# A projection whose next layer norm runs ahead of the group's differences, and an attention stack loaded under two semaphores

## The chip, the cores and the metric

The kernel runs on one core of one Trainium2 chip. A core has five engines that run their own instruction streams: TensorE (PE, with its weight loads shown as PEld), VectorE (DVE), ScalarE (ACT), GpSimd (POOL) and SyncE (SP), which in this kernel issues nearly all DMA transfers. They meet only through semaphores. The metric is the time of one execution in microseconds; less is better. Before the change, three executions took 4418.20, 4414.44 and 4430.01 us, a median of 4418.2 us.

## The reference

The input is x with 4096 rows (2 sequences of 2048) of 256 numbers. Two layers follow one another.

```python
x = x + attention(layernorm(x))      # 16 heads of 16, with relative-position keys and values
x = x + ffn(layernorm(x))            # itself: layernorm, plain attention, layernorm, top-2 of 8 experts
def _layernorm(x, axis=-1, eps=1e-05):
    m = jnp.mean(x, axis=axis, keepdims=True)
    v = jnp.var(x, axis=axis, keepdims=True)
    return (x - m) / jnp.sqrt(v + eps)
q = proj(Wq, bq); k = proj(Wk, bk); v = proj(Wv, bv)          # x @ W.T + b, 16 heads
scores = jnp.einsum('bqhd,bkhd->bhqk', q, k) / np.sqrt(DK)     # plain attention
attn = jax.nn.softmax(scores, axis=-1)
```

## The kernel before, in words

The program is a chain of stages, each a block of its own with its own semaphores; between two blocks the engines meet and SP clears the semaphores of the old one. The order is: first projection (`rel_projection`), attention with relative positions, middle stage, plain attention (`plain_attention`), routing, experts. Inside a block the order of each engine's work is written out by hand, and nothing reorders it.

**First projection.** The 4096 rows are taken in 8 groups of 512 (g = 0 to 7). For each group TensorE
transposes the normalised rows h into psT (L1505), ACT copies them to hT (L1467), TensorE multiplies them with the query and key weights into four banks of psU (L1522) and with the value weights into the two halves of psV (L1537). Queries and keys are stored as two numbers each, a rounded high part and the rest. ACT makes the six high parts of a group (L1483, output rel_parts), one or two for each bank; DVE makes the six differences, value minus high part (L1412, also rel_parts). The differences free the psU banks for the next group. DVE also adds the bias to both halves of psV (L1423, output rel_vout). SP stores each of the six outputs after its difference (L1346), the values after the second vout (L1352), and right behind the first store of group g it loads x for group g+2 (L1350).

The layer norm of the next group is a generator on DVE (`layer_norm`, L91), stepped from between the differences. Its steps are: statistics of four tiles (L94); three sums (L98); mean and square (L101, L102); variance (L106); plus epsilon (L110); after ACT's square root (`root`, L1461) the reciprocal (L113); and the four tiles of h (L119). A tuple says how many steps run behind each difference, (2, 2, 1, 1, 1, 0), and on ACT `root(g + 1)` stands behind the fourth high part.

TensorE's order in a group is: psU in four banks, first half of psV, the transposes of group g+1 (they wait for h), second half of psV. In group 0 the second half of psV also waits for rel_ekt, a copy (L1428) that DVE makes between its two vout additions.

**Plain attention.** 32 heads run one after the other. A head's queries and keys lie in a stack of 128 partitions: the lower rows (from partition 0, 48 of them) serve the first pass, in which TensorE forms scores (L459) only so that DVE can take their maxima (L370); the upper rows (from partition 64, 50 of them) serve the second pass, the fills (L484), whose results ACT turns into exponentials (L433). SP loads a stack with twelve transfers of 128 KB (`load_stacks`, L275): six for the lower rows, then six for the upper. All twelve count up one semaphore of the stack's slot, `s_qz[slot]`; there are four slots. TensorE waits for it once, ahead of the first score of a head. At the start SP issues the stacks of heads 0 and 1, then the values of all heads, then head 2.

Of the kernel before, what the change touches and what calls it, by code (L numbers as in the profile page):

```python
# [16 lines left out]
DK = D // NH  # L17
NB = 2
S = 2048
# [8 lines left out]
NG = T // G  # L28
# [95 lines left out]
U = 4  # L124
HEADS = NB * NH
# [36 lines left out]
def plain_attention(nc, ident, sel, qd, kd, vd, den_d, rec_d, ot_rows):  # L162
# [19 lines left out]
    with ExitStack() as ctx:  # L182
# [28 lines left out]
        psO = ps("psO", [P, G])  # L211

        s_one, s_init, s_vall, s_v = sem("s_one"), sem("s_init"), sem("s_vall"), sem("s_v")
        s_qz = [sem(f"s_qz{i}") for i in range(U)]
        s_a, s_am, s_nm, s_mt, s_mh, s_mr, s_mq = (sem(n) for n in
            ("s_a", "s_am", "s_nm", "s_mt", "s_mh", "s_mr", "s_mq"))
        s_fl, s_ex, s_us, s_oev = (sem(n) for n in ("s_fl", "s_ex", "s_us", "s_oev"))
# [3 lines left out]
        ctx.callback(clear_semaphores, nc, sems)  # L221
        blk = ctx.enter_context(nc.Block())

        NLD = 4 * len(Q2)
        NINIT = 5
        lead = 3

# [34 lines left out]
        @blk.sync  # L262
        def _(sp):
            def load_stacks(t, p):
                b, h = head(t)
                slot = p % U
                row, col = ready(sp, h * DK), ready(sp, b * S)
                s_us.wait(sp, STEPS * (t - 3))
                for half in range(2):
                    if half and t < U:  # L270
                        s_one.wait(sp, t + 1)
                    for parts, dst, src in ((Q2, qs, qd), (K2, zs, kd)):
                        for i, part in enumerate(parts):
                            at = 64 * half + i * DK
                            sp.dma_start(dst[at:at + DK, slot, :].bitcast(F32),  # L275
                                         src[part, bass.ds(row, DK), bass.ds(col, S)]).then_inc(s_qz[slot].h, 16)

            def send_m(t, p):
                s_mr.wait(sp, t + 1)
                for m in range(NP2):  # L280
                    at = 64 + PR + m
                    sp.dma_start(qs[at:at + 1, p % U, :].bitcast(F32), mrow[:, m, :].bitcast(F32)
                                 ).then_inc(s_mq.h, 16)

            def spread_reciprocals(t, n):

                s_nf.wait(sp, t + 1)
                for c in range(4):
                    row = 32 * c + DK
                    sp.dma_start(den_d[:, c * G:(c + 1) * G].rearrange("(a u) q -> a u q", a=1),  # L290
                                 ob[row:row + 1, :, :]).then_inc(s_dw.h, 16)
                s_dw.wait(sp, 64 * (n + 1))
                sp.dma_start(den[:, :], den_d.rearrange("u (x j) -> (u x) j", j=U * S // P)).then_inc(s_dr.h, 16)
                s_rec.wait(sp, n + 1)
                sp.dma_start(rec_d.rearrange("u (x j) -> (u x) j", j=U * S // P), rec[:, :]).then_inc(s_rw.h, 16)
                s_rw.wait(sp, 16 * (n + 1))
                for c in range(4):
                    sp.dma_start(recb[32 * c:32 * c + DK, :, :],
                                 bass.AP(rec_d.tensor, rec_d.offset + c * G, [[0, DK], [S, U], [1, G]])
                                 ).then_inc(s_rr.h, 16)  # L300

            def store_o(t, n):

                b, h = head(t + HEADS - U)
                row, col = ready(sp, h * DK), ready(sp, b * S)
                s_ml.wait(sp, n + 1)
                for c in range(4):
                    sp.dma_start(ot_rows[bass.ds(row, U * DK), bass.ds(col + c * G, G)].rearrange(
                        "(u d) q -> d u q", u=U), done[32 * c:32 * c + DK, :, :]).then_inc(s_ob.h, 16)

            give_credits(sp, sems)
            for t in range(lead):
                load_stacks(t, t)
                if t == 1:
                    for b in range(NB):
                        sp.dma_start(vall[:, b, :, :], vd[b * S:(b + 1) * S, :].rearrange("(z p) c -> p z c", p=P)
                                     ).then_inc(s_vall.h, 16)
            send_m(0, 0)
            for it in range(HEADS // U):
                for p in range(U):  # L320
                    t = U * it + p
                    if t + lead < HEADS:
                        load_stacks(t + lead, p + lead)
                    if p == 0:
                        spread_reciprocals(t, it)
                    if t + 1 < HEADS:
                        send_m(t + 1, p + 1)
                    if p == 0:
                        store_o(t, it)
            for k in range(U):  # L330
                s_qz[k].wait(sp, 16 * NLD * HEADS // U)
            s_mq.wait(sp, 16 * NP2 * HEADS)
            spread_reciprocals(HEADS, HEADS // U)
            store_o(HEADS, HEADS // U)
            s_ob.wait(sp, 64 * (HEADS // U + 1))
# [116 lines left out]
        def _(pe):  # L452
            def scores(a, half, w, p, loaded):

                k, a = p + a // 32, a % 32
                if a == 0 and half == 0:
                    s_qz[k % U].wait(pe, 16 * NLD * loaded(k))
                i, e = a // 2, 2 * (a % 2) + half
                last = pe.matmul(psA[w][:, half, :], qs[0:PR, k % U, i * P:(i + 1) * P],  # L459
                                 zs[0:PR, k % U, e * G:(e + 1) * G], start=True, stop=True)  # L460
                if half:
                    last.then_inc(s_a.h, 1)
# [13 lines left out]
            def fill(t, p, i):  # L476
                if t == HEADS:
                    return
                s_ex.wait(pe, BANKS * t + before(i) + 1)
                if i == 0:  # L480
                    s_mq.wait(pe, 16 * NP2 * (t + 1))
                c, z = i // 16, i % 16
                at = 64
                pe.matmul(psS[:, slot(i), :], zs[at:at + PR + NP2, p % U, z * P:(z + 1) * P],  # L484
                          qs[at:at + PR + NP2, p % U, c * G:(c + 1) * G], start=True, stop=True).then_inc(s_fl.h, 1)
# [784 lines left out]
def rel_projection(nc, A, ident, sel, masks, e_stack, evc, ev_side, q2, kl2, kr2, v_rows):  # L1270
# [10 lines left out]
    with ExitStack() as ctx:  # L1281
# [112 lines left out]
        def _(dve):  # L1394
# [12 lines left out]
            for g in range(NG):  # L1407
                q = g % 2
                ahead = normalise(dve, g + 1) if g + 1 < NG else iter(())
                for o, (m, col, _, _) in enumerate(OUTS):  # L1410
                    s_hi.wait(dve, NO * g + BY_UNIT[m])
                    dve.scalar_tensor_tensor(out=parts[:, q, o, 1, :], in0=psU[:, m, :], scalar=cols[:, col:col + 1],  # L1412
                                             in1=parts[:, q, o, 0, :], op0=ALU.add, op1=ALU.subtract
                                             ).then_inc(s_lo.h, 1)
                    for _ in zip(range((2, 2, 1, 1, 1, 0)[o]), ahead):
                        pass
                for v in range(2):
                    s_v.wait(dve, 2 * g + v + 1)
                    if v == 0:
# [32 lines left out]
        @blk.scalar  # L1452
        def _(act):
            def weight(i, bank):
                s_wt.wait(act, i + 1)
                act.activation(wt[:, :, i * D:(i + 1) * D], bank.rearrange("p (c n) -> p c n", c=CH), ACT.Copy
                               ).then_inc(s_wc.h, 1)

            def root(g):
                s_ve.wait(act, g + 1)  # L1460
                act.activation(sd[:, g % 2, :], ve[:, g % 2, :], ACT.Sqrt).then_inc(s_sd.h, 1)  # L1461

            def stationary(g):
                s_v.wait(act, 2 * (g - 1))
                for c in range(CH):
                    s_t.wait(act, CH * g + c + 1)
                    act.activation(hT[:, g % 2, c, :], psT[:, c, :], ACT.Copy).then_inc(s_hT.h, 1)  # L1467

            weight(0, psU[:, 2, :])
            root(0)  # L1470
            weight(1, psU[:, 3, :])
            stationary(0)
            weight(2, psV[:, 0, :, :].rearrange("p a c -> p (a c)"))
            for g in range(NG):
                q = g % 2
                for o, (m, col, _, _) in enumerate(OUTS):
                    s_u.wait(act, 4 * g + m + 1)
                    if g == 0 and o == 0:
                        s_bias.wait(act, 16 * 6)
                    if g == 0 and col == 4:  # L1480
                        s_col.wait(act, 4)
                    s_po[q][o].wait(act, 16 * (g // 2))
                    act.activation(parts[:, q, o, 0, :], psU[:, m, :], ACT.Identity, bias=cols[:, col:col + 1]  # L1483
                                   ).then_inc(s_hi.h, 1)
                    if o == 3 and g + 1 < NG:
                        root(g + 1)
                if g + 1 < NG:
                    stationary(g + 1)

# [1123 lines left out]
```

## Time and profile before

| quantity | value |
|---|---|
| median of three executions | 4418.2 us |
| the profiled execution | 4430.09 us, span 4428.4 us |
| first projection, in the span | 0 to about 128 us |
| start of plain attention (first load to first score) | 2231.16 to 2245.63 us |
| PE, DVE, ACT, POOL busy over the span | 90%, 79%, 68%, 33% |

A row of the timeline reads: start, duration, engine, line of the program, operation, tile written and tiles read, shapes, how many instructions are merged into the row; in brackets the time for which the engine stood idle before it and what it waited for. The busy shares are means over stages with different limits; what the change is worth is read from the two stretches in the table.

### The profile page before, as it was taken

The numbers are of one execution on the slowest core, as the hardware profiler recorded it, in microseconds if no ns is written. First come the engines' busy times: TensorE is split into PE (matmuls) and PEld (weight loads), VectorE is DVE, ScalarE is ACT, GpSimd is POOL, SyncE is SP. The second block draws the span as 40 slices with busy tenths as digits, with TensorE's granted clock in tenths as the row PEclk, the third lists the DMA queues.
The fourth block names the chain that finished last, engine by engine and source line by source line (L and its number), as shares of the span: only waits on it lengthen the run. The fifth ranks groups of instructions, "written<-read, shape, count | busy, mean of one in ns | idle before, by whom it ended". The sixth has DMA issues, their size and how long they took to land. (4 is left out here: it accounts for less than half of the span.)

```text
span 4428.4 us, 77243 instructions
## 1 busy us (share of the span) xinstructions
PE 4001.6 (90%) x26592; PEld 2106.5 (48%) x26592; DVE 3490.8 (79%) x6304; ACT 2991.0 (68%) x5821; POOL 1445.9 (33%) x1405
## 2 busy tenths in 40 slices
PE   7699999999999999996879999999999996689997
PEld 4344444444444444443533333333333332589997
DVE  6688888888888888862769888988888881577775
ACT  3067777777777777783218888888888884256664
POOL 0255666666666656662100000000000000613222
PEclk9589999999999999998959999999999997689998
DMA  7656666666666767654662323233333302666664
GB/s 269 179 142 164 150 163 161 163 154 168 155 159 159 168 159 165 161 116 129 234 120 40 54 30 54 40 44 45 44 44 46 43 13 70 176 207 174 177 170 115
DMA packets 486195, 556.39 MB, mean 126 GB/s; under 512 B 60260, under 2 KB 426836, under 8 KB 476524
## 3 DMA queue, kind: packets, MB, share of 16 engines
q1 hardware_dynamic: 465980, 526.94, 49.1%
q0 software_dynamic: 19824, 24.52, 3.5%
q8 instruction: 211, 3.46, 0.4%
q14 instruction: 180, 1.47, 0.1%
HBM read 347.67 MB, written 206.76 MB: 125 GB/s over the span
## 5 line engine op out<-in xcount | busy, mean ns | idle before, releaser
L1096 ACT ACTIVATE ra_p<-ra_psS 128x512 f32<-128x512 f32 x2048 | 1089.6, 605 | 368.2 <-PE ra_psS L1173 266.1
L370 DVE TENSOR_REDUCE pa_pm<-pa_psA 128x2 f32<-128x1024 f32 x1024 | 1208.3, 1219 | 140.7 <-PE pa_psA L459 140.7
L1007 DVE TENSOR_REDUCE ra_pm<-ra_psA 128x1 f32<-128x896 f32 x1024 | 1113.5, 1087 | 205.9 <-PE ra_psA L1131 190.4
L433 ACT ACTIVATE pa_p<-pa_psS 128x512 f32<-128x512 f32 x2048 | 1063.5, 604 | 249.4 <-PE pa_psS L484 245.0
L484 PE MATMUL pa_psS<-pa_qs,pa_zs 50*128 50x512 f32 x2048 | 793.4, 464 | 77.3 <-ACT pa_p L433 62.8
L459 PE MATMUL pa_psA<-pa_zs,pa_qs 48*128 48x512 f32 x2048 | 797.2, 472 | 44.2 <-DMA pa_zs<-k_halves 23.8
L1131 PE MATMUL ra_psA<-ra_zs,ra_qs 48*128 48x512 f32 x2048 | 736.0, 455 | 44.9 <-DVE ra_pm L1009 23.8
L1173 PE MATMUL ra_psS<-ra_qs,ra_zs 50*128 50x512 f32 (+3 forms) x2176 | 713.8, 411 | 32.4 <-ACT ra_p L1096 17.5
L484 PEld LDWEIGHTS pa_psS<-pa_qs,pa_zs 50*128 50x128 f32 x2048 | 342.2, 185 | 626.2 <-ACT pa_p L433 606.7
L1204 PE MATMUL ra_psO<-ra_p,ra_vs 128*32 128x512 f32 (+3 forms) x6400 | 566.6, 459 | 0.0
L495 PE MATMUL pa_psO<-pa_p,pa_vs 128*32 128x512 f32 x4096 | 548.0, 607 | 0.0
L1173 PEld LDWEIGHTS ra_psS<-ra_qs,ra_zs 50*128 50x128 f32 x2176 | 353.4, 187 | 395.4 <-ACT ra_p L1096 307.7
L459 PEld LDWEIGHTS pa_psA<-pa_zs,pa_qs 48*128 48x128 f32 x2048 | 346.6, 189 | 214.0 <-DVE pa_pm L370 160.5
L1131 PEld LDWEIGHTS ra_psA<-ra_zs,ra_qs 48*128 48x128 f32 x2048 | 328.5, 194 | 166.4 <-DVE ra_pm L1009 85.0
L343 POOL COPY pa_vs<-pa_vall 128x256 f32<-128x256 f32 x32 | 12.7, 399 | 1057.1 <-PE pa_psO L495 1023.7
L947 POOL TENSOR_TENSOR ra_blk<-ra_blk 128x508 f32<-128x508 f32 x128 | 162.9, 1273 | 461.6 <-DMA ra_blk<-window_rows 456.6
L2353 PE MATMUL mo_psH<-mo_hp,mo_w_parts 128*128 128x384 f32 x1392 | 285.3, 341 | 5.9 <-DVE mo_w_parts L2439 5.9
L2367 PE MATMUL mo_psY<-mo_w_parts,mo_hid_parts 128*128 128x256 f32 x2088 | 283.6, 281 | 0.6 <-DVE mo_hid_parts L2509 0.6
L2324 POOL DMA_INDIRECT acc_rows<-mo_y,mo_ids x87 | 154.5, 1776 | 387.7 <-DVE mo_y L2494 370.0
L2367 PEld LDWEIGHTS mo_psY<-mo_w_parts,mo_hid_parts 128*128 128x128 f32 x2088 | 272.1, 189 | 4.9 <-DVE mo_hid_parts L2509 1.1
L1204 PEld LDWEIGHTS ra_psO<-ra_p,ra_vs 128*32 128x32 f32 x6400 | 194.9, 109 | 131.2 <-ACT ra_p L1096 82.5
L1102 ACT ACTIVATE ra_sw<-ra_sw,ra_nm 128x256 f32<-128x256 f32 x512 | 242.8, 526 | 0.0
(247 smaller groups left out, 4977.9 us busy)
## 6 DMA issues: line engine op xcount, KB each, us to landing
relative_rows<-ra_rst SPq DMA_DIRECT2D x128, 512.0 KB, 4.0
ra_blk<-window_rows SPq DMA_DIRECT2D x128, 512.0 KB
mo_w_raw<-ffn_W SPq DMA_DIRECT2D x58, 1024.0 KB, 5.5
ra_zs<-k_halves SPq DMA_DIRECT2D x192, 248.0 KB, 7.4
ra_dl<-relative_rows SPq DMA_DIRECT2D x128, 256.0 KB, 5.4
window_rows<-ra_pc SPq DMA_DIRECT2D x128, 256.0 KB, 4.8
pa_qs<-q_halves SPq DMA_DIRECT2D x192, 128.0 KB, 6.3
pa_zs<-k_halves SPq DMA_DIRECT2D x192, 128.0 KB, 6.9
```

Source lines behind the costliest of these rows:

```text
L370: dve.reduce_max(pm[:, par, 2 * a:2 * a + 2], psA[w][:, :, :], AX.X).then_inc(s_am.h, 1)
L433: act.activation(pr[:, i % NPR, :], psS[:, slot(i), :], ACT.Exp).then_inc(s_ex.h, 1)
L459: last = pe.matmul(psA[w][:, half, :], qs[0:PR, k % U, i * P:(i + 1) * P], zs[0:PR, k % U, e * G:(e + 1) * G], start=True, stop=True)
L484: pe.matmul(psS[:, slot(i), :], zs[at:at + PR + NP2, p % U, z * P:(z + 1) * P], qs[at:at + PR + NP2, p % U, c * G:(c + 1) * G], start=True ...
L495: last = pe.matmul(psO[32 * m:32 * m + 32, :], vs[:, p % 2, 4 * (k % 4) + m, :], pr[:, (4 * k + m) % NPR, :], start=k % 4 == 0, stop=k % 4 ...
L1007: dve.reduce_max(pm[:, q, i, 2 * left:2 * left + 1], psA[w][:, lo:lo + 2 * G - P], AX.X).then_inc(s_far.h, 1)
L1096: act.activation(dst, psS[:, slot(i), :], ACT.Exp if kind == "E" else ACT.Copy).then_inc(s_cp.h, 1)
L1131: last = pe.matmul(psA[w][:, half * G:(half + 1) * G], qs[0:PR, q, i * P:(i + 1) * P], zs[0:PR, q, at:at + G], start=True, stop=True)
L1173: last = pe.matmul(dst[:, lo:hi], zs[at:at + PR + NP2, q, z * P:(z + 1) * P], qs[at:at + PR + NP2, q, c * G + lo:c * G + hi], start=True, ...
L1204: last = pe.matmul(psO[32 * m:32 * m + 32, lo:hi], v[:, z, :], pr[:, (4 * k + m) % NPR, lo:hi], start=n == 0, stop=n == 3, tile_position=( ...
L2353: last = pe.matmul(psH[:, u % 3, 0:BT], w1[:, q, x, c, f * P:(f + 1) * P], hp[:, q, z, c, :], start=c == 0 and m == 0, stop=c == CH - 1 an ...
L2367: last = pe.matmul(psY[:, j, 0:D], hid[:, x, u % NHID, j * P:(j + 1) * P], w2[:, q, z, f, :], start=f == 0 and m == 0, stop=f == FC - 1 an ...
```

## The change

In `rel_projection` the numbers of layer-norm steps become (5, 2, 0, 0, 0, 0) and the stepping moves ahead of each difference: five steps ahead of the first, the last two ahead of the second. On ACT `root(g + 1)` moves ahead of the six high parts. In `plain_attention` the semaphores `s_qz` are replaced by `s_qa` for a slot's lower rows and `s_qe` for its upper rows, each counting six transfers. TensorE waits for `s_qa` ahead of a head's first score and for `s_qe` ahead of its first fill. SP waits for both at the end.

```diff
-        s_qz = [sem(f"s_qz{i}") for i in range(U)]
+        s_qa, s_qe = ([sem(f"{n}{i}") for i in range(U)] for n in ("s_qa", "s_qe"))
-        NLD = 4 * len(Q2)
+        NLD = 2 * len(Q2)
...
-                                         src[part, bass.ds(row, DK), bass.ds(col, S)]).then_inc(s_qz[slot].h, 16)
+                                         src[part, bass.ds(row, DK), bass.ds(col, S)]).then_inc((s_qe if half else s_qa)[slot].h, 16)
...
-                s_qz[k].wait(sp, 16 * NLD * HEADS // U)
+                s_qa[k].wait(sp, 16 * NLD * HEADS // U)
+                s_qe[k].wait(sp, 16 * NLD * HEADS // U)
...
                 if a == 0 and half == 0:
-                    s_qz[k % U].wait(pe, 16 * NLD * loaded(k))
+                    s_qa[k % U].wait(pe, 16 * NLD * loaded(k))
...
                 if i == 0:
+                    s_qe[p % U].wait(pe, 16 * NLD * (t // U + 1))
                     s_mq.wait(pe, 16 * NP2 * (t + 1))
...
                 for o, (m, col, _, _) in enumerate(OUTS):
+                    for _ in zip(range((5, 2, 0, 0, 0, 0)[o]), ahead):
+                        pass
                     s_hi.wait(dve, NO * g + BY_UNIT[m])
                     dve.scalar_tensor_tensor(out=parts[:, q, o, 1, :], in0=psU[:, m, :], scalar=cols[:, col:col + 1],
                                              in1=parts[:, q, o, 0, :], op0=ALU.add, op1=ALU.subtract
                                              ).then_inc(s_lo.h, 1)
-                    for _ in zip(range((2, 2, 1, 1, 1, 0)[o]), ahead):
-                        pass
...
             for g in range(NG):
                 q = g % 2
+                if g + 1 < NG:
+                    root(g + 1)
                 for o, (m, col, _, _) in enumerate(OUTS):
...
-                    if o == 3 and g + 1 < NG:
-                        root(g + 1)
```

On VectorE, group 1 of the first projection stands so before the change (L1412 is a difference, L94 to L119 are the layer norm of group 2):

```order
L1412 SCALAR_TENSOR_TENSOR rel_parts<-rel_psU,rel_cols,rel_parts 128x512
L94 BN_STATS rel_stats<-rel_x 128x6 x4
L98 TENSOR_TENSOR rel_moments<-rel_stats 128x4 x3
L1412 SCALAR_TENSOR_TENSOR rel_parts<-rel_psU,rel_cols,rel_parts 128x512
L101 TENSOR_SCALAR rel_mean<-rel_moments 128x4
L102 SCALAR_TENSOR_TENSOR rel_moments<-rel_moments 128x4
L106 SCALAR_TENSOR_TENSOR rel_moments<-rel_moments 128x4
L1412 SCALAR_TENSOR_TENSOR rel_parts<-rel_psU,rel_cols,rel_parts 128x512
L110 TENSOR_SCALAR rel_ve<-rel_moments 128x4
L1412 SCALAR_TENSOR_TENSOR rel_parts<-rel_psU,rel_cols,rel_parts 128x512
L113 RECIPROCAL rel_rs<-rel_sd 128x4
L1412 SCALAR_TENSOR_TENSOR rel_parts<-rel_psU,rel_cols,rel_parts 128x512
```

The same group on VectorE after the change (a difference is now L1416, the vout addition L1425):

```order
L94 BN_STATS rel_stats<-rel_x 128x6 x4
L98 TENSOR_TENSOR rel_moments<-rel_stats 128x4 x3
L101 TENSOR_SCALAR rel_mean<-rel_moments 128x4
L102 SCALAR_TENSOR_TENSOR rel_moments<-rel_moments 128x4
L106 SCALAR_TENSOR_TENSOR rel_moments<-rel_moments 128x4
L110 TENSOR_SCALAR rel_ve<-rel_moments 128x4
L1416 SCALAR_TENSOR_TENSOR rel_parts<-rel_psU,rel_cols,rel_parts 128x512
L113 RECIPROCAL rel_rs<-rel_sd 128x4
L119 TENSOR_SCALAR rel_h<-rel_x,rel_mean,rel_rs 128x256 x4
L1416 SCALAR_TENSOR_TENSOR rel_parts<-rel_psU,rel_cols,rel_parts 128x512 x5
L1425 TENSOR_TENSOR rel_vout<-rel_psV,rel_v_bias 128x512 x2
```

The four tiles of h, which stood behind the fifth difference, now stand behind the first; five differences and the vout additions follow in a row.

On ScalarE, groups 0 and 1 before the change (L1483 is a high part, L1461 the square root, L1467 the copy of hT):

```order
L1483 ACTIVATE rel_parts<-rel_psU,rel_cols 128x512 x4
L1461 ACTIVATE rel_sd<-rel_ve 128x4
L1483 ACTIVATE rel_parts<-rel_psU,rel_cols 128x512 x2
L1467 ACTIVATE rel_hT<-rel_psT 128x512 x2
L1483 ACTIVATE rel_parts<-rel_psU,rel_cols 128x512 x4
L1461 ACTIVATE rel_sd<-rel_ve 128x4
```

And after it (the square root is now L1463, a high part L1487, the copy of hT L1469):

```order
L1463 ACTIVATE rel_sd<-rel_ve 128x4
L1487 ACTIVATE rel_parts<-rel_psU,rel_cols 128x512 x6
L1469 ACTIVATE rel_hT<-rel_psT 128x512 x2
L1463 ACTIVATE rel_sd<-rel_ve 128x4
L1487 ACTIVATE rel_parts<-rel_psU,rel_cols 128x512 x6
```

The square root has moved from behind the fourth high part to ahead of the first. In plain attention no instruction that computes or transfers is moved.

## Rows read from the trace of the kernel before

**Rows 1.** Page, the head and one of the costliest groups: idle before it, and releaser.
```profile
span 4428.4 us, 77243 instructions
...
L459 PE MATMUL pa_psA<-pa_zs,pa_qs 48*128 48x512 f32 x2048 | 797.2, 472 | 44.2 <-DMA pa_zs<-k_halves 23.8
```

**Rows 2.** Waits, 0 to 170 us: waiter, releaser, total us, times, longest.
```profile
PE rel_psT L1505 <- DVE rel_h L119: 18.0, 8, 2.4
```

**Rows 3.** Timeline of PE, group 4 of the first projection.
```profile
71.20 7.03 PE L1522 MATMUL rel_psU<-rel_hT,rel_w_qkv_t 128*128 128x512 f32 x16
78.07 1.89 PE L1537 MATMUL rel_psV<-rel_w_qkv_t,rel_hT 128*128 128x256 f32 x8
82.20 1.09 PE L1505 MATMUL rel_psT<-ident,rel_h 128*128 128x128 f32 x8 [2.24 <-DVE rel_h L119]
83.13 1.89 PE L1537 MATMUL rel_psV<-rel_w_qkv_t,rel_hT 128*128 128x256 f32 x8
84.86 7.03 PE L1522 MATMUL rel_psU<-rel_hT,rel_w_qkv_t 128*128 128x512 f32 x16
```

**Rows 4.** Timeline of the other engines in the same group.
```profile
71.40 0.69 DVE L1423 TENSOR_TENSOR rel_vout<-rel_psV,rel_v_bias 128x512 f32<-128x512 f32 x1 [1.66 <-PE rel_psV L1537]
...
73.12 0.69 ACT L1483 ACTIVATE rel_parts<-rel_psU,rel_cols 128x512 fp32r<-128x512 f32 x1 [2.74 <-PE rel_psU L1522]
73.84 0.75 DVE L1412 SCALAR_TENSOR_TENSOR rel_parts<-rel_psU,rel_cols,rel_parts 128x512 fp32r<-128x512 f32 x1 [1.75 <-ACT rel_parts L1483]
...
75.02 0.47 SPq L1350 DMA_DIRECT2D rel_x<-attn_x  x1
...
76.55 1.27 ACT L1483 ACTIVATE rel_parts<-rel_psU,rel_cols 128x512 fp32r<-128x512 f32 x2 [1.03 <-PE rel_psU L1522]
...
82.95 1.08 ACT L1467 ACTIVATE rel_hT<-rel_psT 128x512 f32<-128x512 f32 x2 [2.88 <-PE rel_psT L1505]
```

**Rows 5.** Timeline, middle stage: a layer norm that no difference interrupts.
```profile
2196.26 0.69 DVE L1735 TENSOR_TENSOR mid_vout<-mid_psV,mid_v_bias 128x512 f32<-128x512 f32 x1 [1.91 <-PE mid_psV L1821]
...
2199.31 0.21 ACT L1744 ACTIVATE mid_sd<-mid_ve 128x4 f32<-128x4 f32 x1 [3.72 <-DVE mid_ve L110]
2199.43 1.25 ACT L1768 ACTIVATE mid_parts<-mid_psU,mid_cols 128x512 fp32r<-128x512 f32 x2
2200.13 0.75 DVE L1722 SCALAR_TENSOR_TENSOR mid_parts<-mid_psU,mid_cols,mid_parts 128x512 fp32r<-128x512 f32 x1 [0.85 <-ACT mid_parts L1768]
...
2201.00 1.38 DVE L119 TENSOR_SCALAR mid_h<-mid_x,mid_mean,mid_rs 128x256 f32<-128x256 f32 x4
2202.30 0.74 DVE L1722 SCALAR_TENSOR_TENSOR mid_parts<-mid_psU,mid_cols,mid_parts 128x512 fp32r<-128x512 f32 x1
```

**Rows 6.** Timeline, group 0 of the first projection: the two halves of psV.
```profile
21.55 1.89 PE L1537 MATMUL rel_psV<-rel_w_qkv_t,rel_hT 128*128 128x256 f32 x8
...
27.02 3.37 PE L1537 MATMUL rel_psV<-rel_w_qkv_t,rel_hT 128*128 128x256 f32 x8 [0.24 <-DVE rel_ekt L1428]
```

**Rows 7.** Windows (ending: granted clock, DMA share, GB/s) and the landing of x.
```profile
57.50:71.20 13.70, 11.46 (x41) 6.85 (x41) 8.89 (x24) 5.09 (x9) 0.00 (x0) 1.00 0.88 316
...
66.00:68.00 2.00, 0.30 (x2) 0.00 (x0) 1.55 (x4) 0.41 (x1) 0.00 (x0) 1.00 1.05 408
...
DMA to landing us min/median/max: 4.7/4.7/6.4
```

**Rows 8.** Plain attention's start: the six lower-row loads, and the first score.
```profile
2231.16 1.83 SPq L275 DMA_DIRECT2D pa_qs<-q_halves  x3
...
L275 SPq DMA_DIRECT2D pa_zs<-k_halves x3: 419/420/420, 2233.0 to 2234.0; - x3
...
DMA to landing us min/median/max: 3.0/4.1/5.5
...
2245.63 2.07 PE L459 MATMUL pa_psA<-pa_zs,pa_qs 48*128 48x512 f32 x4 [23.84 <-DMA pa_zs<-k_halves]
```

**Rows 9.** Windows, plain attention: where the granted clock rises.
```profile
2315.00:2325.00 10.00, 9.63 (x52) 3.00 (x54) 6.63 (x7) 6.07 (x13) 0.00 (x0) 0.74 0.01 3
```

## The prediction

> **What bounds the kernel now.** I read the page first: the span, and the group of first-pass score matmuls, whose PE idle time names a DMA as its longest releaser: 23.8 us behind the load of the key stack [rows 1]. That is one wait, at the start of plain attention, where PE, DVE and ACT all stand still. The page's slices show the first projection only as four blurred columns, so I asked for the waits of 0 to 170 us. There TensorE waits 18.0 us in 8 waits for the normalised tile h that VectorE writes [rows 2]. The timeline of TensorE alone shows where [rows 3]: a group runs from one start of the psU matmuls to the next, 71.20 to 84.86, so 13.66 us. In it PE does psU (6.87 us to the next start), half of psV, then stands 2.24 us for h, then transposes (0.93 us to the next start) and the second half of psV (1.73 us). A first half of psV also takes 1.73, so the work in a group is 6.87 + 1.73 + 0.93 + 1.73 = 11.26 us, and 2.40 us of the period is the hole before the transposes. PE is at the full clock there (1.00, which is 2.4 GHz) [rows 7]. The last wait in this stage is thus h, which VectorE finishes late because its six steps stand between six differences. The rest of the program (both attentions, the middle stage, routing, the experts) is touched only through the starting time of plain attention.
>
> **Part 1, the steady group.** The edit adds and removes no arithmetic. It moves the layer norm of group g+1 on DVE ahead of the differences of group g, and the square root on ACT from behind the fourth high part to ahead of the first. I lay out a new group from the start of psU as zero.
> The trace of before has a layer norm that runs undivided, in the middle stage [rows 5]: from the start of the vout addition (2196.26) to the square root on ACT is 3.05 us, and the next ACT high part starts at 3.17. In the projection vout starts at +0.20 [rows 4], so now the root starts at +3.25 and the first high part at +3.37. Before it was at +1.92 (73.12). ACT therefore loses 1.45 us at the front: the price of the edit, because high parts 1 to 6 are queued behind a root that waits for DVE. The first difference follows the high part by 0.72 [rows 4]: +4.09. From a difference to h is 0.87 (2200.13 to 2201.00), h takes 1.38, the next difference starts 2.17 after the first [rows 5]: h is complete at +6.34, the second difference is at +6.26. Differences in a row cost 0.74 each (durations 0.75 with the overlap of starts), so the last starts at +9.2, vout at +9.9, and DVE is done at +10.6. The last two high parts need the fourth bank: banks come 1.715 us apart (76.55 less 73.12, halved), so at +7.07, and two high parts take 1.27: +8.3, ahead of the fifth difference (+8.5). ACT is not late.
> PE ends the first half of psV at +8.60 and finds h ready since +6.34, so the 2.24 us wait is gone with 2.26 to spare. It transposes to +9.53. ACT copies hT from 0.75 after the transposes start, for 1.08 [rows 4], so to +10.43; PE ends psV at +11.26 and finds hT ready. The next psU bank needs only the first difference. DVE meets the next vout at +11.46 with 0.9 us in hand. What is late next is nothing but PE itself: period 11.26, gain 2.40 in each of groups 1 to 6: **14.4 us**. Group 7 has no layer norm behind it and stays.
>
> **Group 0.** Here the second half of psV also waits for a copy (rel_ekt) that stands behind the differences and vout. The fourth bank reaches ACT about 0.2 us after psV's start at 21.55 [rows 6], two high parts end at 23.0, difference 5 at 23.05, difference 6 at 23.8, vout at 24.45, the copy at 25.1 to 25.4. PE starts at 25.4 where it started at 27.02: **1.6 us**. That half of psV took 3.37 us for eight matmuls where 1.89 is usual [rows 3, 6], so PE fell to its lower clock level (1.2 GHz) behind its pause. If the shorter pause keeps it at the upper level, another 1.5 us comes. I take nothing for that, since the only row for this place is the slow one, and keep 1.5 for the low end of the range. DVE still has its constants to make at the start of group 1 (about 2 us); h is then ready at about +8.4, still ahead of +8.60.
>
> **The transfers.** Each group issues seven stores and one load of 512 KB, 4.19 MB. SP passes the x load right behind the first store, now at +5.3 (difference 1 plus the 1.18 us from 73.84 to 75.02) instead of +3.8, and the next statistics want it at +11.26 + 0.20 + 0.69 = +12.15: 6.9 us, where landings take 4.7 to 6.4 [rows 7]. Before, it had some 13 us. The stores no longer have gaps between them but come in a burst. Windows in which the queue is full show 408 GB/s at a share of 1.05 [rows 7]; at 400 GB/s the group needs 10.5 us of the 11.26. It just fits, so I charge nothing.
>
> **Part 2, the stacks.** PE's first score waited for all 12 loads of head 0 and now waits for the 6 of the lower rows. SP issues in the same order. The sixth load is issued at 2234.0 and landed 5.5 us later, at 2239.5 (it is the largest of the six landings); PE started at 2245.63 [rows 8]. That is 6.0 us earlier, less 0.2 that I allow for four more semaphores that SP credits ahead of the loads (no row has a price for one; it is bounded below by nothing and above by 1 us): **5.8 us**. Everything behind it moves along: VectorE sets the pace of the first turns, and its own memsets are over by then. The upper rows are wanted only by the first fill some 56 us later, and have landed. The added wait stands once a head on PE ahead of a fill, with the scores, fills and weighings queued behind it, and its load is three heads old: nothing, at most 0.04 us in each of 32 heads, 1.3 us. Clearing four more semaphores and four more waits of SP at the end: 0.3 us.
>
> **The sum.** 14.4 + 1.6 + 5.8 - 0.3 = 21.5 us. The profiled execution took 4430.1 us (1.7 beside its span), which would become 4408.6. It was the slowest of the executions shown, 12 us above their median of 4418.2 us, so I set the forecast against the median: **4397 us**. The executions of one kernel lie 16 us apart, which is nearly the size of the effect.
>
> **A limit on transfers.** The shares read otherwise than the full windows: over a whole group 316 GB/s at a share of 0.88 is 359 GB/s at a full share [rows 7]. By that a group needs 4.19/0.359 = 11.7 us, the queue becomes the bound at 11.7 instead of 11.26, and groups 1 to 6 give 2.0 each, 11.7 in all. The sum is then 18.8 and the time 4399.
> The Trainium skill, "DMA: Bandwidth & Descriptors", section "Where 436 GB/s comes from", says that a transfer between HBM and SBUF is bound by about 358 GB/s for each core, below the 435 GB/s of the fabric. By that rule the limit above holds and the group takes 11.7 us; the two-microsecond windows of this trace go above it, and an average of the changed stage over some groups will tell.
>
> **Rivals.** (a) The forecast, 4388 to 4405: 0.60. (b) The transfers bind as above, 4399: 0.15. For it is the mean share, against it the full windows. (c) The stacks bring nothing net: PE runs at the lower level from its first score to about 2318, where the window 2315 to 2325 shows 0.74 [rows 9]. Fills begin 56 us after the first score, and PE is dense from then. If the rise stays at its old time while work comes 5.8 us sooner, 5.8 us more of dense work runs at half speed, which costs 2.9, and a like shift at the start of relative attention up to as much. Gain 16, time 4402: 0.15. (d) The projection does not do what it says, since DVE, not PE, sets the period: it has 0.9 us in hand, and if every semaphore hop in the longer chain vout, statistics, root, high part, difference, h costs more than in the middle stage it can need 13 us. Then only part 2 and about 1 us are left: 4412: 0.06. (e) Slower: the x load comes late. Its deadline is 6.9 us after issue, PE has 2.26 more, so it hurts from 9.1 us of landing, and groups 2 to 6 (those fed by the five loads issued inside the loop) only equal the old period at 11.5. The whole kernel is slower from 13.4 us. At 18 us, four times today's 4.7, each of the five groups loses 18 - 11.5 = 6.5 us, 32 in all, against 9.5 gained elsewhere: 4441. The burst of stores in one queue speaks for it, the shorter queue that a longer period would leave speaks against it: 0.04.
>
> **Numbers.** What a measurement of this kernel can tell from no change is about 0.5%, 22 us, and the forecast of 21.5 stands almost on it. Of (a) 0.37 lies beyond it, with the clock's 1.5 us and the spread of executions, of the others 0.05, by the spread alone: faster 0.42, within 0.54, slower 0.04. The range is 4387 (all of it, the 1.5 us and a fast median) to 4412 (case d); it leaves out (e) and the tails of (a).
>
> **What would show it.** In the profile after: psU starts of groups 1 to 7 11.3 us apart; no wait of rel_psT for rel_h; the ACT root before all six high parts, its wait for ve grown to about 1.5 us or more; the first difference about 4.1 us after psU starts; DMA share near 1 in the stage; the last matmul of the projection near 106.5 us instead of 122.7; the first score of plain attention 8.7 us after its first load is issued, instead of 14.5 (2231.16 to 2245.63) [rows 8]. The prediction is wrong if the period stays above 12, if the first score comes later than 10 us behind the first load, or if later stages give the time back.

## The result, and the profile after

Twelve executions of the changed kernel took 4403.2 us in the median (4380.46 to 4426.22), twelve of the kernel before 4434.5 (4414.44 to 4460.02). The ratio is 0.993 with a 95% interval of 0.9909 to 0.9951: 31 us faster, 22 to 40. The forecast was 21.5 us, and 4397 us for the time. A second comparison on another chip (below) gave 0.9949, 22.6 us, and the places in the trace add up to 22.0. So the mechanism was sized rightly, and some 9 us of the first comparison belong to neither part of the change. The time itself came out near the forecast partly by luck: the median of before that it started from, 4418.2 us of three executions, is 16 us below that of twelve, and the gain was 10 us above the forecast. Where such scatter comes from is the second half of this text; for the first comparison itself it can't be shown, since the executions of the kernel before there have, but for one, no clock on record. The profiled execution has a span of 4401.8 us, 26.6 less than before.

First the projection. Timeline of PE, group 4 of the changed kernel, answering to [rows 3]:

```profile
60.62 7.03 PE L1524 MATMUL rel_psU<-rel_hT,rel_w_qkv_t 128*128 128x512 f32 x16
67.48 1.89 PE L1539 MATMUL rel_psV<-rel_w_qkv_t,rel_hT 128*128 128x256 f32 x8
69.21 1.04 PE L1507 MATMUL rel_psT<-ident,rel_h 128*128 128x128 f32 x8
70.08 1.89 PE L1539 MATMUL rel_psV<-rel_w_qkv_t,rel_hT 128*128 128x256 f32 x8
71.81 7.03 PE L1524 MATMUL rel_psU<-rel_hT,rel_w_qkv_t 128*128 128x512 f32 x16
```

The bracket behind the transposes is gone: PE no longer waits for h here. From psU to psU it is 11.19 us instead of 13.66. The other engines in the same group, answering to [rows 4]:

```profile
63.23 1.41 DVE L94 BATCH_NORM_STATS2 rel_stats<-rel_x 128x6 f32<-128x256 f32 x4 [1.72 <-DMA rel_x<-attn_x]
...
65.69 0.20 ACT L1463 ACTIVATE rel_sd<-rel_ve 128x4 f32<-128x4 f32 x1 [5.89 <-DVE rel_ve L110]
65.80 3.56 ACT L1487 ACTIVATE rel_parts<-rel_psU,rel_cols 128x512 fp32r<-128x512 f32 x6
66.50 0.75 DVE L1416 SCALAR_TENSOR_TENSOR rel_parts<-rel_psU,rel_cols,rel_parts 128x512 fp32r<-128x512 f32 x1 [0.85 <-ACT rel_parts L1487]
...
67.38 1.38 DVE L119 TENSOR_SCALAR rel_h<-rel_x,rel_mean,rel_rs 128x256 f32<-128x256 f32 x4
...
67.69 0.81 SPq L1352 DMA_DIRECT2D rel_x<-attn_x  x1
68.67 3.38 DVE L1416 SCALAR_TENSOR_TENSOR rel_parts<-rel_psU,rel_cols,rel_parts 128x512 fp32r<-128x512 f32 x5
...
71.97 1.28 DVE L1425 TENSOR_TENSOR rel_vout<-rel_psV,rel_v_bias 128x512 f32<-128x512 f32 x2
```

The root follows the start of the statistics by 2.46 us and the first difference by 3.27; the forecast, from the middle stage's undivided norm, had 2.36 and 3.20. But the statistics themselves start at +2.61 and not at +0.9, since DVE waits 1.72 us for x. h is thus ready at +8.14, 0.45 us ahead of PE instead of 2.26. In group 5 nothing is left:

```profile
78.98 1.38 DVE L119 TENSOR_SCALAR rel_h<-rel_x,rel_mean,rel_rs 128x256 f32<-128x256 f32 x4
...
80.42 1.09 PE L1507 MATMUL rel_psT<-ident,rel_h 128*128 128x128 f32 x8
```

h is complete at 80.36, the transposes start 0.06 us later (as in the kernel before, where PE waited: 68.48 and 68.54), and this one group takes 11.27 us. In three other profiles with this order (part 1 alone, the changed kernel again, the interleaved middle stage) every group takes 11.2 us and h is at least 0.99 us ahead from group 2 on.

The wait for x is new, and it feeds itself. SP issues the load behind the first difference, and that now stands behind statistics that wait for the load before. From one start of the statistics to the next it is 3.27 us to the difference, 1.19 to the issue (67.69) and 6.3 to 7.3 more to the next statistics: 11.8, 11.6 and 10.8 us in groups 3 to 5, around the period of 11.2. Windows, one group (granted clock, DMA share and GB/s at the end), and DVE's waits of 27 to 104 us (total, times, longest), of the changed kernel:

```profile
60.60:71.80 11.20, 11.20 (x41) 6.91 (x40) 8.46 (x24) 4.76 (x9) 0.00 (x0) 1.00 1.03 373
```

```profile
DVE rel_stats L94 <- DMA rel_x<-attn_x: 5.2, 4, 1.7
```

The queue carries 373 GB/s at a share of 1.03, where [rows 7] had 316 at a share of 0.88. That settles the rival in which transfers bind at 359 and the period is 11.7: the queue carries a group in 11.2 us. That it has next to nothing to spare is read from the share, and no run tests it. At the end of the stage the burst shows as well. Last store and first matmul of relative attention, changed kernel:

```profile
106.06 1.25 SPq L1354 DMA_DIRECT2D v_rows<-rel_vout  x1
...
128.60 2.08 PE L1143 MATMUL ra_psA<-e_stack,ra_qs 48*128 48x256 f32 x8 [23.84 <-DMA ra_zs<-k_halves]
```

From the start of the last value matmul (104.38) to that first matmul, three profiles with the old order take 22.8, 23.4 and 22.8 us, three with the new order 24.2, 23.6 and 23.9: 0.9 us given back to stores that are still queued.

The start of plain attention, changed kernel, answering to [rows 8]:

```profile
2208.68 1.16 POOL L350 MEMSET pa_vs<- 128x1024 f32 x2 [48.97 <-POOLq L68]
...
2210.55 1.27 SPq L275 DMA_DIRECT2D pa_qs<-q_halves  x3
...
2218.74 2.07 PE L460 MATMUL pa_psA<-pa_zs,pa_qs 48*128 48x512 f32 x4 [17.79 <-DMA pa_zs<-k_halves]
```

8.19 us from the first load to the first score, where it was 14.47. The first load stands 1.87 us behind POOL's first memset, where the kernel before had 1.65: 0.22 us for the four semaphores.

### The profile page after: what moved, and what is told of

Read it like the earlier page. It is cut to its first block and busy times, and to the rows that moved or that the text cites. A ratio compares the mean times of both kernels' runs of the same rounds, so it can differ in the third digit from the quotient of the medians.

```text
span 4401.8 us, 77253 instructions
## 1 busy us (share of the span) xinstructions
PE 3988.2 (91%) x26592; PEld 2101.9 (48%) x26592; DVE 3491.7 (79%) x6304; ACT 2990.7 (68%) x5821; POOL 1447.8 (33%) x1405
## 5 line engine op out<-in xcount | busy, mean ns | idle before, releaser
L371 DVE TENSOR_REDUCE pa_pm<-pa_psA 128x2 f32<-128x1024 f32 x1024 | 1208.4, 1219 | 134.7 <-PE pa_psA L460 134.7
```

Of the source, the lines that this page charges most:

```text
L371: dve.reduce_max(pm[:, par, 2 * a:2 * a + 2], psA[w][:, :, :], AX.X).then_inc(s_am.h, 1)
```

## The experiments

### Each part alone, an idle change, and the whole again

The first kernel has only the first part of the diff, the second only the second. The third is the kernel before with one line more, the fourth the changed kernel as it is. All on one chip.

```diff
+        idle = [sem(f"s_idle{i}") for i in range(U)]
```

> The first part alone (layer norm and root ahead), plain attention as before. Theory A (each part saves what its own stage shows, the rest of the change in time is the clock of relative attention, which varies from one execution to the next): last value matmuls of the projection at 101.1 us as in the changed kernel, first matmul of relative attention near 128.6, plain attention's first score 14.5 us after its first load; 16.5 us faster than before, ratio 0.9963. Theory B (the earlier end of the projection also changes how often the clock falls in relative attention, every time): 20 to 26 us faster, and again fewer than 70 us at the lower level between 270 and 1980 us, where the profile of before has 85 us. Theory C (the parts work only together): under 5 us.

> The second part alone (a semaphore each for lower and upper rows), projection as before. Theory A: first score 8.2 to 8.5 us after the first load instead of 14.5, 6.1 us faster than before, and 0 to 2 us more if the clock rises sooner behind it; ratio 0.9984. Theory B: the same, since nothing ahead of it moves. Theory C: under 1 us, if the first fills or the clock give it back. Group 0 of the projection again has its second half of psV at 3.4 us, at the lower level.

> The kernel before with four more semaphores in plain attention that are credited and cleared, and which nobody waits for. It prices the semaphores and is the comparison of two kernels that do the same. Expected: first load of plain attention 0.1 to 0.3 us later behind the memsets, time within 0.15% of before (ratio 0.9985 to 1.0015) if the spread of executions averages out over five rounds. Theory B says that the time at the lower level in relative attention stays at the 85 us of the profile of before; theory A lets it be anything from 55 to 100.

> The changed kernel once more, beside the other three on the same chip. Theory A: 22.6 us faster than before (16.5 + 6.1), ratio 0.9949, and the time at the lower level in relative attention is not the 65 us of its first profile. Theory B: 26 to 31 us faster again, and 65 us at the lower level. The sum of the two single parts should equal it within 6 us under A.

| kernel | median us | ratio, 95% interval | start of psU in group 1 to start of the last value matmul, us | first load to first score, us | low clock in relative attention, us |
|---|---|---|---|---|---|
| before (first profile) | 4421.5 | | 92.1 | 14.5 | 85 |
| part 1 alone | 4400.2 | 0.9957, 0.9941 to 0.9973 | 77.3 | 14.5 | 79 |
| part 2 alone | 4412.2 | 0.9979, 0.9963 to 0.9995 | 92.1 | 8.3 | 123 |
| idle semaphores | 4426.5 | 1.0017, 0.9999 to 1.0035 | 92.0 | 14.3 | 140 |
| changed, again | 4398.3 | 0.9949, 0.9929 to 0.9969 | 77.3 | 8.3 | 72 |

The fourth column and the fifth take two values each: each part does its work alone, in its own place, and the two add up (19.0 + 9.3 against 22.6, within the intervals). Theory C falls. The last column is the time at the lower level, 1.2 GHz, between the first rise of the clock in that stage and its last maxima. A kernel in which nothing ahead of or in relative attention is changed has 85 us in one execution and 140 in another; theory A had allowed no more than 100. These five rows alone would still fit theory B, since both kernels with the new order have less than the three with the old. The profiles of the later experiments speak against it: there the projection also ends early (103.6 to 105.0 us), and they have 150, 123, 79 and 130 us. So do whole executions: the mean time at the lower level (worked out below) is 527 us before and 541 with idle semaphores, 513, 513 and 520 for part 1, part 2 and both, each with an interval of 8 to 13 us either way; on the next chip it is 553 before and 554 with a reordered projection. A regular effect of the order on the clock is not seen; one of a few us in the time is not excluded.

That clock explains the times. In ten profiles (both kernels and the single experiments) the length of relative attention is 1747.3 us plus 0.36 us for each us at the lower level, within 3.5 us, over a span of 28 us. (The 1743.5 us in an expectation below goes with times at the lower level that were read 10.6 us too long, the clock's marks and the instructions having been counted from different zeros.) For whole executions each result lists span and mean granted clock, so 2 x (1 - clock) x span is the time at the lower level. Over 137 executions on three chips, one slope of 0.40 us per us, with a constant for each kernel and chip, leaves a spread of 2.0 us, where the spans of one kernel on one chip are up to 50 us apart. At equal time at the lower level, with 95% intervals of that fit:

| kernel | against before, us | with the 2.5 us below |
|---|---|---|
| idle semaphores | -0.1 +- 1.3 | |
| part 1 alone | -14.4 +- 1.3 | |
| part 2 alone | -3.6 +- 1.3 | -6.1 |
| changed, again | -19.3 +- 1.3 | -21.8 |

One correction belongs to it. The 6.2 us that part 2 removes are idle time at the lower level, so the fit credits 0.40 of them to the clock; 2.5 us are to be added back. Then part 2 (6.1) and the whole (21.8) agree with the places in the trace (5.8 and 22.0, added up below), and the null is a null. Part 1 (14.4) comes out 1.8 us below its places (16.2), just outside its interval; why stays open.

### What had to be ahead, and what the load of x can do

In the first, the root stays behind the fourth high part; in the second, x is loaded behind the sixth store. There is one execution of each, so only their stages are read, not their times.

```diff
-                if g + 1 < NG:
-                    root(g + 1)
+                    if o == 3 and g + 1 < NG:
+                        root(g + 1)
```

```diff
-                    if o == 0 and 3 <= g + 2 < NG:
+                    if o == NO - 1 and 3 <= g + 2 < NG:
```

> The changed kernel, but the square root on ACT stays behind the fourth high part, as before. DVE's order is the new one. Theory A (PE is the bound and anything that has h ready before 8.6 us will do): the first high part is back at +1.9, root at about +6.65, h complete at about +8.5, period of a group 11.2 to 11.4 us, and DVE's wait for x gone since the statistics start later. Theory B (the root has to be ahead, else DVE sets the period, since five differences are queued behind h): period 12.5 to 13.5 us, PE waits for h again.

> The changed kernel, but SP passes the load of x behind the sixth store instead of the first. Theory A (the load is the link that turns the change into a loss, as in the rival that ends slower): statistics, differences, sixth store, load and landing form a loop of about 9.5 + 1 + 5 to 6 us, period of groups 2 to 6 is 15 to 16.5 us, above the 13.66 of before, PE waits 3.5 to 5 us for h, projection's end about 8 to 15 us later than before's 122.3. Theory B (x has slack to spare): period stays below 11.5.

With the late root the period is 11.20 us, as in the changed kernel. ACT and DVE of this kernel, same group:

```profile
67.83 0.20 ACT L1463 ACTIVATE rel_sd<-rel_ve 128x4 f32<-128x4 f32 x1
68.07 0.18 DVE L113 RECIPROCAL rel_rs<-rel_sd 128x4 f32<-128x4 f32 x1 [2.12 <-ACT rel_sd L1463]
68.28 1.38 DVE L119 TENSOR_SCALAR rel_h<-rel_x,rel_mean,rel_rs 128x256 f32<-128x256 f32 x4
```

h is ready at 69.66, 8.33 us behind psU's start at 61.33, and PE wants it at 8.6. So in the steady groups the move of the root was not needed; DVE waits 2.12 us for it where it has waited for x before. What counts there is that h beats PE, not by how much. In group 0 the move did count. The second half of psV, changed kernel, then with the late root:

```profile
25.20 1.99 PE L1539 MATMUL rel_psV<-rel_w_qkv_t,rel_hT 128*128 128x256 f32 x8 [0.87 <-DVE rel_ekt L1430]
```

```profile
25.91 1.99 PE L1539 MATMUL rel_psV<-rel_w_qkv_t,rel_hT 128*128 128x256 f32 x8 [2.73 <-DVE rel_ekt L1430]
```

Measured from the first half (21.56 and 20.41) it starts 3.64 us behind in the one and 5.50 in the other: 1.9 us once, since DVE's wait for the root delays the copy rel_ekt too. Before the change it was 5.47 us (21.55 to 27.02), so the late root gives back all that the copy had gained.

The late load is where the projection turns into a loss. Timeline of that kernel:

```profile
73.88 1.28 SPq L1352 DMA_DIRECT2D rel_x<-attn_x  x1
...
80.61 1.41 DVE L94 BATCH_NORM_STATS2 rel_stats<-rel_x 128x6 f32<-128x256 f32 x4 [6.55 <-DMA rel_x<-attn_x]
...
86.06 3.38 DVE L1416 SCALAR_TENSOR_TENSOR rel_parts<-rel_psU,rel_cols,rel_parts 128x512 fp32r<-128x512 f32 x5
86.20 1.97 PE L1507 MATMUL rel_psT<-ident,rel_h 128*128 128x128 f32 x8 [4.27 <-DVE rel_h L119]
...
91.31 1.25 SPq L1352 DMA_DIRECT2D rel_x<-attn_x  x1
```

Groups take 17.0 to 18.7 us, and the projection's last matmul comes at 134.7 us, 12.4 later than before the change. (The whole execution took 4432.4 us against a median of 4438.5 before, with the stacks' gain in it; at equal clock 3.4 +- 4.0 us more than before, which tells nothing.) The loop can be read off: 6.7 us from issue to statistics, 8.8 to the end of the sixth difference (89.44), 1.9 until SP is through four stores: 17.4. I had expected 15 to 16.5; the shape is right, SP and the landing took 2 us more. PE also drops to its lower level behind these waits: its transposes take 1.97 us instead of 1.04. The price of the load, named in the rival that ends slower, is real. It is the loop that the changed kernel has too, there at 10.8 to 11.8 us; it stays clear of the price by 0.45 us of h in group 4 and by nothing in group 5.

### Orders that might be better

The first has the first difference ahead of the norm again, the second reorders the middle stage, the third has both.

```diff
-                    for _ in zip(range((5, 2, 0, 0, 0, 0)[o]), ahead):
+                    for _ in zip(range((0, 5, 2, 0, 0, 0)[o]), ahead):
...
-                if g + 1 < NG:
-                    root(g + 1)
+                    if o == 1 and g + 1 < NG:
+                        root(g + 1)
```

```diff
-                for o, steps in enumerate((5, 2, 5, 0)):
+                for o, steps in enumerate((2, 3, 2, 5)):
...
-                    if g + 1 < NG and o in (0, 3):
-                        root(2 * (g + 1) + (o == 3))
+                    if g + 1 < NG and o == 2:
+                        root(2 * (g + 1))
...
                 if g + 1 < NG:
+                    root(2 * (g + 1) + 1)
                     stationary(g + 1)
```

> The changed kernel with the first difference ahead of the layer norm again: steps (0, 5, 2, 0, 0, 0), and on ACT the root behind the second high part. Theory A (PE is the bound): h complete at about +8.1, period 11.2 us as in the changed kernel, no wait of DVE for x; the stores are spread a little, so relative attention may start up to 0.9 us sooner behind the last matmul; time within 0.15% of the changed kernel. Theory B (DVE has no time left for a wait of 1.8 us ahead of its first difference): period 11.5 to 12.2 us, 2 to 6 us slower than the changed kernel.

> The changed kernel, and the middle stage reordered: its layer norm steps go from (5, 2, 5, 0) to (2, 3, 2, 5) ahead of the four differences, the roots on ACT to ahead of the third high part and behind the fourth. There psU has two banks only, so that TensorE waits about 3 us in each group for the first difference, which stands behind five steps. Theory A (ahead is right only where no bank waits for a difference): that wait falls under 0.5 us, period of a group from 19.6 to 15 to 16.5 us, stage 20 to 28 us shorter, ratio to before 0.988 to 0.991. Theory B (something else sets the middle stage: the residual, POOL's addition, the DMA): under 7 us.

> Both reorderings together: the projection with its first difference ahead of the layer norm, and the interleaved middle stage. Theory A (places add up, the rest is the clock): projection period 11.2 us, relative attention's first matmul 22.9 us behind the last matmul of the projection and not 24, from relative attention's last maxima to the middle stage's last matmul 242 us instead of 258.7, plain attention's first score 8.3 us behind its first load; that is 22.6 + 1 + 16.3 = 40 us faster than before, ratio 0.991, and at least 1 us better than the middle stage's change alone. Theory B (the gains of the middle stage were a lucky execution): ratio near 0.995. In both, the length of relative attention follows 1743.5 us plus 0.36 us for each us that PE stands at the lower clock level in it, within 4 us.

First difference ahead: 0.996 (0.9936 to 0.9985). The period is 11.20 us, DVE no longer waits for x in the loop, and relative attention starts 22.9 us behind the last matmul, so the 0.9 us of the tail are back, and h is a steady 0.72 us ahead of PE. Group 0 gives 0.8 us of that away, since the copy rel_ekt comes later. From the first half of psV (20.03) to the second it is 4.47 us instead of 3.64:

```profile
24.50 1.99 PE L1539 MATMUL rel_psV<-rel_w_qkv_t,rel_hT 128*128 128x256 f32 x8 [1.70 <-DVE rel_ekt L1430]
```

At equal clock this kernel is 18.4 +- 1.4 us (20.9 corrected) ahead of before; against the changed kernel on another chip that is no measurable difference, as expected.

The middle stage has two psU banks for four products. PE there, changed kernel, one group:

```profile
2135.76 3.60 PE L1813 MATMUL mid_psU<-mid_hT,mid_w_qkv 128*128 128x512 f32 x8
2142.59 5.39 PE L1813 MATMUL mid_psU<-mid_hT,mid_w_qkv 128*128 128x512 f32 x8 [3.23 <-DVE mid_parts L1724]
```

The same order that helps the projection (five steps ahead of the first difference) makes PE wait here 3.23 us for the bank. PE with the interleaved middle stage:

```profile
2125.93 7.14 PE L1814 MATMUL mid_psU<-mid_hT,mid_w_qkv 128*128 128x512 f32 x16
...
2138.67 1.09 PE L1794 MATMUL mid_psT<-ident,mid_h 128*128 128x128 f32 x8 [0.41 <-DVE mid_h L119]
...
2141.33 7.14 PE L1814 MATMUL mid_psU<-mid_hT,mid_w_qkv 128*128 128x512 f32 x16
```

The wait is gone, 0.4 to 1.2 us for h have come in its place. The stage's groups take 16.0 us on average instead of 18.2, and from relative attention's last maxima to the stage's last matmul it is 242.3 us instead of 258.7 (259 to 261 us over the nine profiles with the old middle stage): 16.3 us, less than the 20 to 28 expected, since I had taken one of the longer groups (19.6) for the mean. The ratio to before is 0.9909 (0.9876 to 0.9942), at equal clock -33.9 +- 1.8 us, 36.4 corrected. The changed kernel was not run on this chip; the kernel with the first difference ahead was, and at equal clock the interleaved middle stage is 15.5 us ahead of it. Both together: 0.9905 (0.9874 to 0.9936), at equal clock -33.6 +- 2.0, 36.1 corrected, where 40 were expected. The middle stage's order beats both kernels of this case. The extra us in the projection can't be told, and by its places it is 0.1 us: 0.9 at the tail less 0.8 in group 0, which the expectation overlooked. The length of relative attention in the last profile, 1827.0 us with 223 us at the lower level, lies on the line above (1827.5).

## Why the prediction was right

**Steady groups**, forecast 14.4 us: from the start of psU in group 1 to the last value matmul the stage fell from 92.1 to 77.3 us in every profile, 14.7 us. PE became the bound, as worked out; the transposes cost it 0.87 instead of 0.93. Not foreseen was DVE's wait of up to 1.7 us for x, which used up most of the slack of 2.26 us and in group 5 all of it. The prediction gave the load a fixed 6.9 us from an issue at +5.3. But the load stands behind the first difference, so every wait for x also delays the next load: it went out at +7.07. Nothing was lost but 0.07 us; that the margin sufficed was close.

**Group 0**, forecast 1.6 and perhaps 1.5 more: the profiles gave 3.2, but the profile of before was the slowest of three. The copy is done 1.8 us earlier. The slow second half of psV does not come every time: with the same order it took 3.37 us before, 2.77 in part 2 alone (behind transposes of 1.92 us), and 1.99 with idle semaphores. Here, that kernel:

```profile
25.57 1.99 PE L1538 MATMUL rel_psV<-rel_w_qkv_t,rel_hT 128*128 128x256 f32 x8 [0.35 <-DVE rel_ekt L1429]
```

In all eight profiles with a changed projection it took 1.99. So the 1.5 us that the prediction kept for its low end look real in two executions of three; three profiles are few for it. From psU to psU, group 0 takes 16.1 us on average over three profiles with the old order, and 13.7 over the five with the new one: 2.4 us, with 1.5 us of scatter either way.

**The transfers**, forecast at nothing: the one term of the sum that failed, by 0.9 us at the stage's end. I compared a group's bytes with the queue's rate, and did not ask what is still queued when the last group ends.

**The stacks**, forecast 5.8 us: 6.2 us in three pairs of profiles, less 0.22 us for the semaphores ahead of the loads (0.2 was allowed).

**The sum**: 2.4 + 14.7 - 0.9 + 6.2 - 0.4 = 22.0 us. (0.4 is the semaphores twice, 0.22 us ahead of the loads and about as much at the stage's end: from its last instruction to the next stage 14.3 to 14.5 us with them, 14.2 without.) Forecast 21.5. Of the rivals, the limit on transfers and DVE as the bound fall by the period of 11.2 us; the loss through the clock behind the stacks did not show (the rise came 66 to 71 us behind the first score with part 2 and 67 to 75 without); the late load was shown by forcing it.

The 26.6 us between the two profiles divide into 17.9 at the projection's last matmul, 16.5 at relative attention's first, 20.8 at its last maxima (65 us at the lower level against 85), 26.9 at plain attention's first score, 28.8 once the clock had risen there, and 26.6 at the end. Only the first, second and fourth of these steps are the change's; the rest came and went with the clock. What makes the clock fall in one execution and not in another stays open.

## What to carry to other kernels

Ask of a layer norm or any look-ahead work what waits for its result and what waits for the work behind it. In the projection, with a bank for every product, it could stand ahead of all evictions or behind the first without a difference that could be measured; in the middle stage, with two banks for four products, it had to stand between them. A faster stage packs the same transfers tighter: check the deadline of each load, whether its issue hangs behind work that waits for the load before, and what is still queued at the stage's end. And before reading a fraction of a per cent, put the executions on a line against their granted clock: an effect of 6 us showed clearly where raw times scattered by 30 to 50.

## What was not expected of the hardware

- In relative attention PE stood at the lower level for 93 to 109 us from its first matmul in all eleven profiles, with PE busy most of that time, and the rise in plain attention came 66 to 75 us behind the first score, though PE was busy for 17.2 to 18.5 of every 20 us from 2222 to 2282 in the changed kernel. Windows of the changed kernel, the granted clock third from the end:

```profile
2222.00:2242.00 20.00, 18.53 (x33) 7.90 (x32) 18.60 (x17) 0.00 (x0) 0.00 (x0) 0.50 1.03 205
...
2282.00:2302.00 20.00, 19.32 (x112) 6.13 (x107) 15.38 (x14) 13.33 (x27) 0.00 (x0) 0.82 0.02 4
```

- Three tiny additions on DVE took 2.04 us instead of 0.32 while POOL ran an addition over 128x1024. That the one delayed the other is read from their overlap; no run took POOL's addition away. Middle stage, changed kernel:

```profile
2157.37 2.35 POOL L1678 TENSOR_TENSOR mid_rb<-mid_res,mid_bo 128x1024 f32<-128x1024 f32 x1 [17.27 <-DMA mid_res<-attn_x]
2157.84 2.04 DVE L98 TENSOR_TENSOR mid_moments<-mid_stats 128x4 f32<-128x4 f32 x3
```

- The SP queue carried 373 GB/s over a whole group at a share of 1.03, above the 359 that the shares before suggested, and above the limit of about 358 GB/s for each core that the Trainium skill gives ("DMA: Bandwidth & Descriptors", section "Where 436 GB/s comes from"). The trace does not agree with that limit, and the measurement decides for this kernel, which runs on one core.
